# The sums of later values in four column tiles, and both of their pieces in the last step of a period

## The reference

```python
sc = jnp.where(causal, sc, NEG_INF)
m = jnp.max(sc, axis=-1, keepdims=True)
e = jnp.exp(sc - jnp.where(jnp.isfinite(m), m, 0.0))
e = jnp.where(causal, e, 0.0)
denom = jnp.sum(e, axis=-1, keepdims=True)
probs = e / jnp.where(denom == 0.0, 1.0, denom)
...
attn_probs = jax.nn.softmax(attn_scores, axis=-1)
attn_out = jnp.einsum('bhqk,bhkd->bhqd', attn_probs, v)
```

## Time and profile before

| | |
|---|---|
| median of 3 runs | 2356.11 us (2353.27 to 2359.1) |
| the profiled execution, its own time | 2358.39 us |
| its span in the trace | 2356.6 us |
| PE busy | 2206.2 us (94%) |
| DVE, ACT, POOL busy | 1753.1, 1541.6, 1137.6 us |

### The profile page before, as it was taken

The page is one execution under the profiler, slowest core; times in us unless marked ns, Lnnn a source line. Parts: engine busy times, 40 slices in busy tenths (PEclk is TensorE's granted clock), DMA queues, the critical chain, the costliest instruction groups (busy, mean ns, idle before and its releaser), DMA issues.

```text
span 2356.6 us, 46649 instructions
## 1 busy us (share of the span) xinstructions
PE 2206.2 (94%) x19164; PEld 1247.1 (53%) x19164; DVE 1753.1 (74%) x2115; ACT 1541.6 (65%) x2157; POOL 1137.6 (48%) x1070
## 2 busy tenths in 40 slices
PE   6889889999999999999998999999999999989988
PEld 4434334455555555455554655545555555545557
DVE  7786887768787676886778777776877767788466
ACT  2477677766667667676777766776666766667741
POOL 3153133545755456644576257653576544443630
PEclk9999999999999999999999999999999999999999
DMA  5233122311122113121133102231022211101000
GB/s 188 62 109 94 48 55 71 94 48 33 54 68 84 52 35 90 41 68 52 35 90 95 47 20 59 66 108 48 8 70 77 84 35 46 39 19 29 6 27 25
DMA packets 114064, 140.20 MB, mean 59 GB/s; under 512 B 8648, under 2 KB 86760, under 8 KB 113856
## 3 DMA queue, kind: packets, MB, share of 16 engines
q1 hardware_dynamic: 113856, 137.23, 20.5%
HBM read 74.26 MB, written 58.74 MB: 56 GB/s over the span
## 4 chain that ended last, share of the span: by engine, by line
PE 77%; DVE 10%; ACT 5%; POOL 4%; issue 2%; DMA 1%; SPq 0%; ACTq 0%; POOLq 0%
PE pv L800 11%; PE ring L750 9%; PE sums L790 9%; PE score L775 9%; PE score L720 9%; PE sums L732 8%; PE score L673 5%; PE score L688 4%; DVE e L1180 4%; PE ring L829 4%; DVE negmax L1158 3%; PE ring L753 2%; PE score L778 2%; PE score L664 2%; ACT e L1041 2%
## 5 line engine op out<-in xcount | busy, mean ns | idle before, releaser
L1041 ACT ACTIVATE e<-score 128x512 f32<-128x512 f32 x1152 | 672.7, 595 | 372.8 <-PE score L778 207.6
L1180 DVE TENSOR_TENSOR e<-ring,e 128x1024 f32<-128x1024 f32 x576 | 681.2, 1224 | 278.1 <-PE ring L829 277.5
L1158 DVE TENSOR_REDUCE negmax<-ring 128x8 f32<-128x1024 f32 x576 | 681.7, 1219 | 150.7 <-PE ring L753 139.4
L1046 ACT ACTIVATE e<-e 128x2048 f32<-128x2048 f32 x288 | 548.6, 1905 | 4.9 <-DVE e L1180 4.9
L775 PE MATMUL score<-q_st,k_st 112*128 112x512 bf16 (+3 forms) x1536 | 459.5, 330 | 57.3 <-ACT e L1041 22.5
L750 PE MATMUL ring<-k_st,q_st 96*128 96x512 bf16 (+3 forms) x1664 | 387.5, 318 | 39.1 <-DVE e L1180 18.1
L1488 POOL TENSOR_SCALAR r_p<-r_b,ab 128x256 bf16<-128x256 f32 x96 | 89.6, 934 | 544.5 <-DVE r_b L1186 544.5
L800 PE MATMUL pv<-e,v 128*17 128x512 f32 (+3 forms) x3072 | 314.4, 497 | 1.3 <-DVE o_t L1196 1.3
L790 PE MATMUL sums<-e,d_ones 128*32 128x256 f32 x4608 | 305.1, 383 | 1.4
L775 PEld LDWEIGHTS score<-q_st,k_st 112*128 112x128 bf16 x1536 | 147.9, 97 | 248.9 <-issue 122.7
L1467 POOL TENSOR_TENSOR gT<-gT 128x512 f32<-128x512 f32 x112 | 117.2, 1051 | 331.5 <-ACT gT L1014 331.5
(11 more groups left out here) (147 smaller groups left out, 2574.9 us busy)
## 6 DMA issues: line engine op xcount, KB each, us to landing
q_st<-q_parts SPq DMA_DIRECT2D x31, 768.0 KB, 5.9
k_st<-k_parts SPq DMA_DIRECT2D x31, 768.0 KB, 8.6
q_parts<-qk_p SPq DMA_DIRECT2D x30, 384.0 KB, 2.6
k_parts<-qk_p SPq DMA_DIRECT2D x28, 384.0 KB, 2.6
x_in<-in_x SPq DMA_DIRECT2D x8, 1024.0 KB, 5.7
q_parts<-qk_p SPq DMA_DIRECT2D x30, 256.0 KB, 2.9
x_res<-in_x SPq DMA_DIRECT2D x30, 256.0 KB, 4.1
k_parts<-qk_p SPq DMA_DIRECT2D x28, 256.0 KB, 2.9
```

The lines of the kernel that those rows point to most:

```text
L1041: act.activation(e[:, n % ES, hh, :], score[SCORE_SLOT["st", n, hh][0]][:, :], ACT.Exp, scale=DK ** -0.5).then_inc(e1_done, 1)
L1046: act.activation(v, v, ACT.Exp).then_inc(e2_done, 1)
L1158: dve.tensor_reduce(negmax[:, hh:hh + heads, at:at + NB // heads], slot[:, :].rearrange("p (h a n) -> p h a n", h=heads, n=P), AX_X, ALU.m ...
L1180: dve.tensor_tensor(v, ring[no % 2][:, :].rearrange("p (i n) -> p i n", i=2), v, ALU.mult).then_inc(ring_free, 1)
```

## The change

Four things change. BH uses the four groups of 32 columns of the array: block j goes to rows 32 (j mod 4) on, with a stationary operand of 32 columns, so that the seven matmuls leave four partial sums, in 128 rows. ACT copies all 128 rows, to the first half of o_t (which holds outputs only from the taking of the products to their turning). BT joins the four partial sums while it turns them: 16 matmuls, one for each head, with 17 stationary columns and 8 moving ones (a 0/1 matrix `eight`), each into the rows of its head in the group; four column tiles again. Two waits come with the place in o_t: ACT waits for the last turning of outputs before it copies, and DVE waits for BT's matmuls before it writes the first half of o_t. Third, in the tables BH and BT of the periods 1 to 6 leave steps 30 and 31 and both go to step 35, places 0 and 1; F1 number 11, which stood in (35, 0), goes to (34, 1), in the periods 1 to 7; for batch 1, in period 0, BH goes from step 25 to 26, and BT to place 1 of step 26. Fourth, the bias b_out is kept once and read twice, which takes one DVE operation from the prologue.

```diff
-FRONT = {..., (29, 0): ('V', 3), (30, 0): ('BH', 0), (31, 0): ('BT', 0)}
+FRONT = {..., (29, 0): ('V', 3), (35, 0): ('BH', 0), (35, 1): ('BT', 0)}
-BACK = {..., (33, 0): ('F1', 10), (35, 0): ('F1', 11), (38, 0): ('F1', 12), ...}
+BACK = {..., (33, 0): ('F1', 10), (34, 1): ('F1', 11), (38, 0): ('F1', 12), ...}
...
-FIRST[25, 0] = ("BH", 1, 0)
-FIRST[26, 0] = ("BT", 1, 0)
+FIRST[26, 0] = ("BH", 1, 0)
+FIRST[26, 1] = ("BT", 1, 0)
...
+PIECE_STEP = {piece: n for n in range(LAST) for piece in placed(n) if piece}
+
+def last_turned(n):
+    done = [turned_out(k)[0] for k in range(n) if turned_out(k)]
+    return done[-1] if done else None
+
+def last_summed(n):
+    done = [r for r in range(B) if PIECE_STEP["BT", r, 0] < n]
+    return done[-1] if done else None
...
+    for i in range(NB):
+        c[i::32, C_8 + i] = 1.0
...
-        own_rows = slice(QH * MROWS, QH * MROWS + NB)
-        suf_t = m_sb[own_rows, :].bitcast(F32).rearrange("i (h c) -> i h c", h=H)
+        suf_p = o_t[:, 0:BANK].rearrange("p (h c) -> p h c", h=H)
...
                     for j in range(1, NB):
-                        mm = pe.matmul(ps[own_rows, 0:H * VW], u_ind[:, NB - 1 - j:2 * NB - 1 - j], v1[:, r % 2, j, :, :].rearrange("p h c -> p (h c)"),
-                                       start=(j == 1), stop=(j == NB - 1))
+                        own = slice(32 * (j % 4), 32 * (j % 4) + 32)
+                        mm = pe.matmul(ps[own, 0:H * VW], u_ind[:, NB - 1 - j:NB + 31 - j], v1[:, r % 2, j, :, :].rearrange("p h c -> p (h c)"),
+                                       start=(j <= 4), stop=(j >= 4), skip_group_check=True)
                 elif kind == "BT":
                     piece_done(pe, "BH", r, 0)
                     for g in range(NQ):
-                        mm = pe.transpose(ps[:, NB * g:NB * g + NB], suf_t[:, QH * g:QH * g + QH, :].rearrange("i h c -> i (h c)"), id_f[own_rows, own_rows])
+                        for hh in range(QH):
+                            mm = pe.matmul(ps[32 * hh:32 * hh + VW, NB * g:NB * g + NB], suf_p[:, QH * g + hh, 0:VW], eight[:, :],
+                                           start=True, stop=True, skip_group_check=True)
...
                 elif kind == "BH":
-                    act.copy(suf_t[:, :, 0:VW], ps[own_rows, 0:H * VW].rearrange("i (h c) -> i h c", h=H)).then_inc(piece_evac, 1)
+                    out_no = last_turned(PIECE_STEP[item])
+                    if out_no is not None:
+                        act.wait_ge(ring_ready, RING_NO["o", out_no, 0] + 1)
+                    act.copy(suf_p[:, :, 0:VW], ps[:, 0:H * VW].rearrange("p (h c) -> p h c", h=H)).then_inc(piece_evac, 1)
...
+                if half == 0 and last_summed(n) is not None:
+                    piece_full(dve, "BT", last_summed(n), 0)
...
-            for k in range(2):
-                ins = dve.tensor_tensor(b_out[0:3, D * k:D * k + D], b_a[0:3, :], b_h[0:3, :], ALU.add)
-            ins.then_inc(bias_step, 1)
+            dve.tensor_tensor(b_out[0:3, :], b_a[0:3, :], b_h[0:3, :], ALU.add).then_inc(bias_step, 1)
```

More of the change, by code:

```diff
@@ L78 @@
 OUT_AT = 7
[L82 to L83 removed]
+FRONT = {(2, 1): ('T1', 0), (1, 0): ('T1', 1), (1, 1): ('T1', 2), (5, 0): ('T1', 3), (3, 1): ('QK', 0), (5, 1): ('QK', 1), (6, 0): ('QK', 2), (13, 0): ('QK', 3), (15, 0): ('QK', 4), (16, 1): ('QK', 5), (17, 0): ('QK', 6), (15, 1): ('V', 0), (19, 1): ('QK', 7), (24, 0): ('V', 1), (21, 1): ('V', 2), (29, 0): ('V', 3), (35, 0): ('BH', 0), (35, 1): ('BT', 0)}
+BACK = {(8, 0): ('AT', 0), (8, 1): ('AT', 1), (9, 0): ('AT', 2), (12, 0): ('AT', 3), (10, 0): ('O', 0), (11, 0): ('O', 1), (12, 1): ('O', 2), (14, 0): ('O', 3), (18, 0): ('T2', 0), (18, 1): ('T2', 1), (20, 1): ('T2', 2), (24, 1): ('T2', 3), (19, 0): ('F1', 0), (20, 0): ('F1', 1), (21, 0): ('F1', 2), (23, 0): ('F1', 3), (26, 1): ('F1', 4), (27, 0): ('F1', 5), (27, 1): ('F1', 6), (28, 0): ('F1', 7), (32, 0): ('F1', 8), (32, 1): ('F1', 9), (33, 0): ('F1', 10), (34, 1): ('F1', 11), (38, 0): ('F1', 12), (39, 0): ('F1', 13), (40, 0): ('F1', 14), (40, 1): ('F1', 15)}
 QUANTA = {22: (3, 1, 0, 0), 23: (0, 0, 1, 1), 25: (1, 0, 2, 0), 26: (0, 2, 3, 0), 28: (0, 1, 0, 1), 29: (1, 1, 1, 2), 31: (2, 1, 1, 2), 32: (1, 0, 1, 0), 34: (1, 1, 1, 0), 35: (0, 1, 1, 2), 37: (1, 1, 0, 1), 38: (2, 0, 3, 0), 41: (1, 2, 0, 2), 43: (2, 2, 0, 0), 44: (1, 0, 1, 1), 36: (0, 0, 0, 1), 42: (0, 0, 2, 0), 30: (0, 0, 1, 0), 24: (0, 0, 1, 1), 45: (0, 0, 0, 1), 40: (1, 0, 0, 0)}
@@ L295, in columns @@
     return out
-C_ID, C_MQ, C_MT, C_SEL, C_DS, C_U, C_AB, C_OH = 0, 128, 256, 384, 390, 428, 444, 448
+C_ID, C_MQ, C_MT, C_SEL, C_DS, C_U, C_AB, C_8, C_OH = 0, 128, 256, 384, 390, 428, 466, 470, 480
 C_END = C_OH + S
@@ L390, in build @@
         b_qk = sb("b_qk", [P, 2, NT])
-        b_out = sb("b_out", [P, 2 * D], BF16)
+        b_out = sb("b_out", [P, D], BF16)
         one = sb("one", [P, 1], BF16)
@@ L406, in build @@
         d_ones = sb("d_ones", [P, 31 + 2 * TRI])
-        u_ind = sb("u_ind", [P, 2 * NB - 1])
-        own_rows = slice(QH * MROWS, QH * MROWS + NB)
-        suf_t = m_sb[own_rows, :].bitcast(F32).rearrange("i (h c) -> i h c", h=H)
+        u_ind = sb("u_ind", [P, NB - 2 + 32])
+        eight = sb("eight", [P, NB])
+        suf_p = o_t[:, 0:BANK].rearrange("p (h c) -> p h c", h=H)
         ef = e[:, :, :, :].rearrange("p s h n -> p (s h n)")
@@ L669, in tokens_by @@
                 if bias is not None:
-                    pe.matmul(ps, one[:, :].to_broadcast([P, P]), bias[:, :], start=True, stop=False, skip_group_check=True)
+                    pe.matmul(ps, one[:, :].to_broadcast([P, P]), bias[:, :].unsqueeze(1).to_broadcast([P, 2, D]), start=True, stop=False, skip_group_check=True)
                 for i in range(2):
@@ L1323, in _ @@
             dve.tensor_copy(d_ones[:, :], c_sb[:, C_DS:C_DS + 31 + 2 * TRI])
-            dve.tensor_copy(u_ind[:, :], c_sb[:, C_U:C_U + 2 * NB - 1])
+            dve.tensor_copy(u_ind[:, :], c_sb[:, C_U:C_U + NB - 2 + 32])
+            dve.tensor_copy(eight[:, :], c_sb[:, C_8:C_8 + NB])
             dve.tensor_copy(ab[:, :], c_sb[:, C_AB:C_AB + 4])
```

2 lines of the change are left out of this document (removed).

## The result

The changed kernel takes 2342.48 us (median of 5 runs, 2340.14 to 2345.65) against 2356.11 us. The ratio is 0.9937, with a 95% interval of 0.9925 to 0.9948: 13.6 us or 0.6% less. A later set of runs gave 2343.82 against 2357.86 (0.9942, 0.9926 to 0.9959). The profiled execution took 2340.14 us.

What follows compares the result with a forecast made beforehand. PE was taken as the bound, with DVE bounding step 30 once BH leaves. Terms of -3.2 (six periods), -4.6 (period 0) and -4.0 (period 7) sum to -11.8 us on 2358.39, giving 2346.6; forecast 2345 us, range 2337 to 2353.

Steps and rivals of the forecast that it cites:

- Steps 30 and 31: Regular periods without BH and BT: -1.77 us a period, bounds 1.4 and 2.1, DVE bounding step 30.
- F1 11 in step 34: The moved piece lies on PE's path in full in seven periods: +1.75 us each.
- Step 35: Six periods: F1 11 leaves -1.78, wait -0.35, BH +1.02, BT +0.60; sum -0.51 us a period.
- The idle stretch for the square: Step 35: PE's wait for POOL's square of F1 11 goes, 0.19 us idle, 0.35 in all.
- the gain of step 35 goes to another wait: Rival: DVE's chain or late ring buffers take the gain, six periods give -0 to +2, 2349 us; chance 0.17.
- Period 0: First period: shorter BH in step 6 and BH out of step 25, together -4.6 us, bounds -3 and -5.5.
- Period 7: Last period: no wait for the square and no half-clock stretch behind it, -4.0 us, bounds -2.8 and -5.5.
- it all counts: Period 7: PE is busy nearly to the end behind the idle stretch, so the whole -4.0 us shortens the run.
- Serial small tiles: Rival: BT's small tiles do not overlap, 2.65 us a BT, +12 to +14, about 2358 us; chance 0.10.
- the slower case: Rival: BT at 0.113 us a record takes 3.6 us, +19 us, 2364 us; chance 0.05.
- BH without overlap: Rival: BH's column tiles do not overlap, 2.3 us more in 7 places, 2361 us; chance 0.02.
- More than expected: Rival: half-clock stretches fall where PE does less, 0.9 us or more each, 2340 us; chance 0.10.

Runs made afterwards that it cites:

- the last kernel of the table: Kernel before with column tiles for BH and BT at their old places, F1 11 moved in period 7 only, QK 5 first in step 16: 2339.1 us.

## Why the prediction was right, point by point

Forecast 2345 (2337 to 2353); measured 2342.5. Its sum was -11.8 us on the profiled execution, its steps gave -13.3. That it came so near is in part luck: one term holds for another reason than the one given, and errors of some 1.5 us either way cancel.

**Steps 30 and 31**, forecast -1.77 a period: -1.92. The first part, 1.46, was read off period 0, where the same step has no BH, and held to 0.01 us. Step 31 gave 0.46 and not 0.34; the waiting for the delayed ring was not there. The reason given, that DVE is full in this step, is only half right: the windows show DVE busy for 5.96 of 7.21 us, and the run with the statistics moved shows that its load does not matter, only its chain from the r on.

**F1 11 in step 34**, forecast +1.75: +1.98. Mis-sized by 0.2 us. The piece takes 1.83 us and starts 0.21 us behind the last matmul of the scores, where scores follow one another at 0.06: its weight load waits for ACT to have read the bank (0.33 us idle, ended by ACT's L1066). Over seven periods that is 1.5 us too little.

**Step 35**, forecast -0.51: -0.67. BH was forecast at 1.02 and took 1.05. BT was forecast at 0.60, from rounds of four tiles at the price of one serial record, and took 0.31: the largest error in one term, 1.7 us too much in six periods. By these two prices the step should give 0.77; 0.10 of it did not come. The rule of the Trainium skill that spoke against it ("TensorE: Matmul & The Clock Gate", on the 56 ns gap, no start within about 25 ns of the last) would have given 0.8 us; 32 records in 0.31 us are 10 ns each, so that floor does not hold across column tiles. It may hold for each of them: a round of four starts takes 25 ns in six of the seven rounds that can be read, 40 in the first, if a round is the four tiles once, as the groups of 4, 4, 3 and 3 in BH's seven matmuls suggest. The forecast's own argument against the floor was none, since the 61 ns a record of the earlier trace rows are more than 25. The idle stretch for the square went, as forecast.

**One step failed in its reason, not in its number.** I held the square L1467 to blame for DVE's slow stretch, expected the normalisations to get shorter without it, and took 0.6 us for that. The chain did get 0.65 us shorter, but the normalisations did not (2.77 us). The first of the four took 1.09 us beside the square, and takes 1.14 beside the addition of spikes that now stands in its place. The stall of the small product came from POOL's operation ahead of the square, which ends with it at 1144.14:

```profile
1142.99 1.15 POOL L1481 TENSOR_TENSOR acc<-acc,below 128x512 f32<-128x512 f32 x1
```

DVE's L1151 runs from 1143.16 to 1144.16. In the changed kernel that product starts 0.02 us ahead of POOL's addition and takes 0.17. So by the timelines the change gained its 0.67 us because both engines' phases moved against each other, and not because a square fewer stands there: luck. With F1 11 half a step earlier the same chance went the other way and PE waited 1.94 us. The forecast's rival "the gain of step 35 goes to another wait" was nearer than its 0.17 says: DVE's chain allows 8.03 us and PE takes 8.03.

**Period 0**, forecast -4.6: -5.4, since steps 6 and 7 gave 2.1 and not 1.7, and steps 25 to 28 gave 3.3 and not 2.9. **Period 7**, forecast -4.0: 3.3 up to the last denominators and 1.0 behind them, -4.3. The sign given for its step 35, about 7.6 us, forgot that F1 11 leaves the step: it takes 5.20. Of the two stretches at 1.2 GHz the first is gone, and with it the 1.0 us. The second is left, and begins 1.5 us behind a wait of 2.22 us for DVE:

```profile
2233.93 0.70 PE L754 MATMUL sums<-w_proj,gT 128*128 128x256 f32 x2 [2.22 <-DVE r_b L1209]
...
2236.17 2.08 PE L754 MATMUL sums<-w_proj,gT 128*128 128x256 f32 x4
```

It costs nothing. In the second profile of the changed kernel the same wait (2.21 us) stands with no stretch behind it, and the part behind the last denominators takes 108.50 us, against 108.52 with it. So the forecast's "it all counts" does not hold for this stretch, nor does its bound of -5.5.

**The rivals.** Serial small tiles, the slower case and BH without overlap are out, by 0.31 and 1.05 us. "More than expected", by the clock, is partly what happened: the mean clock was 0.991 to 0.992 against 0.990, worth by the fit 1 us of the 13.6, and 2 of the 14.0 in the second set. What the forecast did not see at all is how much the clock can take: at the old places the same tiles lose 7 us to it, by the fit.

## What to carry to other kernels

Price a step without a piece from the same step elsewhere in the program where the piece is missing: that reading was exact. Where two engines arrive within 0.1 us of each other, a gain on one is worth nothing by itself; make room on the other too. As the normalisations put first did: the same move turns from a loss of some 4 us into a gain of some 5 (by the steps; the medians say 14 and 4, with the clock in them). Before believing a difference of under 0.5% in a kernel that is bound by PE, put the mean granted clock beside each time, and compare at equal clock.

## What the runs showed of the hardware

**Matmuls in column tiles.** Sixteen float32 matmuls of 17 stationary and 8 moving columns, in four column tiles, take 0.28 to 0.31 us, as 32 records with 3 to 9 ns from start to start and one gap of 20 (in the changed kernel; repeated four times over, up to 25). In BH the four tiles of a round start 6 to 7 ns apart and the rounds 209 to 235 ns: four matmuls of 272 columns in the time of one. The one-tile form took 3.30 us for the same 14 records.

**DVE behind POOL.** A product of DVE with two inputs, of 8 columns, takes 0.17 us alone. Over the 14 profiles 25 of them start inside a TENSOR_TENSOR of POOL: all take 1.00 to 1.16 us and end 0.02 to 0.03 us after it. The Trainium skill, "SBUF — State Buffer", on the two separate sides, describes a pair of ports that whoever comes first holds for the whole instruction, and the trace agrees for POOL's TENSOR_TENSOR. Not for its TENSOR_SCALAR: of 70 that start inside one, 65 take 0.17 us and five, all in one kernel, 0.46. In the changed kernel one starts at 1132.69, inside the first below, and takes 0.17 us.

```profile
1131.67 1.49 POOL L1505 TENSOR_SCALAR below<-n 128x512 bf16<-128x512 f32 x1
1133.24 1.17 POOL L1507 TENSOR_TENSOR acc<-acc,below 128x512 f32<-128x512 f32 x1
```

**The clock.** The 14 profiles have 126 stretches of PE at 1.2 GHz between step 3 of period 0 and the last microseconds, of 3.4 us, of 6.8, and one of 10.2. Within the 4 us before each of them there is an idle stretch of PE of 0.8 to 2.6 us. But they do not come each time: step 16 has the same waits in every regular period, and the profiled executions show a stretch there in 1 to 6 of six periods, depending on edits made elsewhere. In step 16 one of 3.4 us costs 1.3 to 1.7 us, one of 6.8 us 2.6 to 2.7; where PE is not what the step waits for, as behind period 7, it costs nothing. A new wait of 1.9 us (F1 11 first in step 34) drew one in four of five periods. Why one program draws more of them than another with the same waits is not settled by these runs. There is a hint in their starts: in the last kernel of the table they begin 7.4, 7.2, 7.0, 6.8 and 6.6 us into step 16 of five successive periods, as if they kept a beat of their own, which the length of a period slides past. That would make the length of a period matter, and no run here changed that alone. That the clock differs from program to program, and not by chance alone, is shown by two kernels with the tiles at their old places, which ran at 0.984 to 0.990 in two sets, and the changed kernel, at 0.990 to 0.993 in two; a third kernel with the tiles at the old places, QK 5 first, ran at 0.987 to 0.993.
